# Constant exponential scale from powers of two on q and k, and a reordered front, in an attention and mixture-of-experts kernel

## The reference, cut to what matters

```python
x  = L0_attn_x                     # (B, S, D) = (4, 1024, 128)
xn = layernorm(x, eps=1e-5)
Q = rope(heads(xn @ W_q.T));  K = rope(heads(xn @ W_k.T));  V = heads(xn @ W_v.T)   # 16 heads of 8
attn = softmax(Q @ K.T / sqrt(8))  # full, 1024 x 1024 for each head
a = merge(attn @ V) @ W_o.T
# feed-forward: 8 experts, the top 2 for each row of xn
w, idx = top_k(xn @ Wg, 2);  w = softmax(w)
h_e = relu((norm(xn) * gamma_e + beta_e) @ W1_e + b1_e)
f = sum over the two experts of w_e * (h_e @ W2_e + b2_e + xn)
out = x + a + f
```

## Time and profile before

| | |
|---|---|
| median of 3 runs | 660.07 us (659.75 to 661.24) |
| the profiled execution: time | 659.6 us |
| its span | 657.7 us |
| PE busy | 608.5 us (93%) |
| ACT busy | 548.6 us (83%) |
| DVE busy | 384.1 us (58%) |
| POOL busy | 226.1 us (34%) |

### The profile page before, as it was taken

One profiled execution on the slowest core, in us unless ns is written; L12 is line 12 of the kernel. 1 busy time (PEld: TensorE's weight loads), 2 busy tenths in 40 slices (PEclk: granted clock), 3 DMA queues, 4 the chain that ended last, 5 costly groups with the idle time before them and its releaser, 6 DMA issues.

```text
span 657.7 us, 12339 instructions
## 1 busy us (share of the span) xinstructions
PE 608.5 (93%) x4649; PEld 256.8 (39%) x4649; DVE 384.1 (58%) x1117; ACT 548.6 (83%) x552; POOL 226.1 (34%) x261
## 2 busy tenths in 40 slices
PE   8789889988999999999999999999999999888884
PEld 6223312213545454434454545443444545111112
DVE  4854687888555555587655555558765564335112
ACT  2678899998788888888888888888888888999993
POOL 4399900027753433332433343333234221100000
PEclk9989999999999999999999999999999999999997
DMA  6156411002201202000220120200012111530000
GB/s 229 27 164 179 117 32 33 1 9 53 61 18 29 57 29 57 25 21 17 57 62 17 30 57 29 57 25 21 17 53 54 29 21 45 225 137 32 1 1 34
DMA packets 25425, 35.60 MB, mean 54 GB/s; under 512 B 5472, under 2 KB 15760, under 8 KB 24848
## 3 DMA queue, kind: packets, MB, share of 16 engines
q1 hardware_dynamic: 19936, 23.70, 11.9%
q0 software_dynamic: 4608, 9.45, 5.0%
q10 hardware_dynamic: 816, 1.61, 0.7%
HBM read 17.43 MB, written 8.91 MB: 40 GB/s over the span
## 4 chain that ended last, share of the span: by engine, by line
PE 63%; ACT 22%; DVE 8%; issue 2%; SPq 2%; DMA 1%; DVEq 1%; POOL 0%; ACTq 0%
PE acc L613 23%; ACT ring L825 22%; PE bank L665 11%; PE sc L580 11%; PE bank L657 9%; PE bank L650 2%; PE bank L511 2%; SPq L303 2%; PE bank L674 1%; DVE xn L1169 1%; DVE turned L1148 1%; DVE work L1182 1%; DVE rotated L867 1%; DMA wr<-L_attn_W_k 1%; DVE hl L863 1%
## 5 line engine op out<-in xcount | busy, mean ns | idle before, releaser
L825 ACT ACTIVATE ring<-sc,exp_scale 128x1024 f32<-128x1024 f32 x512 | 534.5, 1130 | 83.2 <-PE sc L580 82.3
L613 PE MATMUL acc<-ring,v 128*9 128x512 f32 x2048 | 268.8, 597 | 2.5 <-issue 2.5
L580 PE MATMUL sc<-qs,ks 32*128 32x512 f16 x1024 | 147.2, 386 | 28.6 <-ACT ring L825 27.4
L456 POOL DMA_INDIRECT token_out<-work,token x72 | 78.4, 1089 | 155.4 <-DVE work L1189 149.1
L446 POOL DMA_INDIRECT work<-normed,token x72 | 70.1, 973 | 159.2 <-DVE work L1175 95.0
L580 PEld LDWEIGHTS sc<-qs,ks 32*128 32x128 f16 x1024 | 40.0, 91 | 145.3 <-ACT ring L825 110.7
L665 PEld LDWEIGHTS bank<-xn,work 128*128 128x128 f32 x576 | 69.7, 191 | 65.1 <-DVE work L1182 37.7
L1182 DVE TENSOR_SCALAR work<-bank,xn 128x128 f32<-128x128 f32 x288 | 80.9, 343 | 22.9 <-PE bank L657 22.8
L665 PE MATMUL bank<-xn,work 128*128 128x128 f32 x576 | 83.2, 287 | 3.1 <-DVE work L1175 3.0
L657 PE MATMUL bank<-work,xn 128*128 128x128 f32 x576 | 77.2, 277 | 2.1 <-DVE norms L888 1.3
L1169 DVE COPY xn<-w_all 128x1158 f32 x72 | 56.5, 785 | 33.2 <-DVE work L1189 32.3
(11 more groups left out here) (175 smaller groups left out, 336.5 us busy)
## 6 DMA issues: line engine op xcount, KB each, us to landing
w_all<-L_ffn_W SPq DMA_DIRECT2D x16, 256.0 KB, 4.9
qs<-hl SPq DMA_DIRECT2D x60, 64.0 KB
ks<-hl SPq DMA_DIRECT2D x60, 64.0 KB
x<-L_attn_x SPq DMA_DIRECT2D x4, 512.0 KB, 7.9
normed<-xn SPq DMA_DIRECT2D x4, 512.0 KB, 3.3
xn<-token_out SPq DMA_DIRECT2D x2, 1024.0 KB, 6.8
w_all<-token_out SPq DMA_DIRECT2D x2, 1024.0 KB, 11.6
out<-x SPq DMA_DIRECT2D x8, 256.0 KB, 2.3
```

Source lines behind the costliest of these rows:

```text
L456: pool.indirect_dma_start(out=y_d[:, :], in_=ys[done % TILE_BUFFERS], in_offset=None, out_offset=bass.IndirectOffsetOnAxis(ap=token[:, 1, ...
L580: last = nc.tensor.matmul(dst, ks[r:r + 32, kb * P:(kb + 1) * P], qs[r:r + 32, at], start=True, stop=not slow)
L613: last = nc.tensor.matmul(acc[qh % 2][32 * j:32 * j + VW, :], v9[:, b, kb, 4 * g + j, :], ring[:, (2 * n + j // 2) % UNITS, j % 2, :], sta ...
L825: nc.scalar.activation(ring[:, (2 * n + u) % UNITS, :, :], sc[u][:, :].rearrange("p (h c) -> p h c", h=2), ACT.Exp, scale=exp_scale[:, 0:1 ...
```

## The change

Both powers of two are now chosen so that their product is 2^14 where there is room for it. The exponential's scale is then the constant 1/(sqrt(8)·2^14), written into the instruction. `exp_scale`, `ungain` and `bound_scale` are gone. `missing` is the factor that k lacks where there was no room; then `no_room` makes the first flag zero, and the general path, which has an additional copy of q and k in `wide`, multiplies what is missing. Its scores run on `wide`.

Beside that the front is reordered: fewer warm-up matmuls; of piece 0 the plain projection comes before the rotated one, for PE and for DVE; the rotated projection of piece 3 comes behind the head norms; the plain projection of piece 2 is made before the flag is read, not in step 0; the moments of batches 2 and 3 are taken at steps 3 and 5; the top-2 of the first batch at step 8 and not 4. POOL makes -mean/std for each row (`offsets`, two small operations) and norms rows as x·a + b; it clears `shift` at the very start, and sorts `wo` before the low halves. `gates` has one operation less.

```diff
-GAIN_EXPONENT = 127 + 12 + 63
+SCORE_BITS = 14
+TOP_EXPONENT = 127 + 12 + 63
-WARM = (10, 18)
+WARM = (10, 12)
-TOP_AT = {4: 0, 11: 1, 15: 2, 19: 3}
+MOMENTS_AT = {3: 2, 5: 3}
+TOP_AT = {8: 0, 11: 1, 15: 2, 19: 3}
...
# POOL
+            nc.gpsimd.memset(shift[:, :], 0.0).then_inc(shift_zero, 1)
...
+            def offsets(ts):
+                after(nc.gpsimd.tensor_tensor(small[:, 9, ts], mv[:, ts, 0], small[:, 6, ts], ALU.mult))
+                after(nc.gpsimd.tensor_scalar(small[:, 8, ts], small[:, 9, ts], -1.0, None, ALU.mult))
...
-                nc.gpsimd.tensor_scalar(xn[:, t, :], x[:, t, :], mv[:, t, 0:1], small[:, 6, t:t + 1],
-                                        ALU.subtract, ALU.mult).then_inc(xn_pool, 1)
+                nc.gpsimd.tensor_scalar(xn[:, t, :], x[:, t, :], small[:, 6, t:t + 1], small[:, 8, t:t + 1],
+                                        ALU.mult, ALU.add).then_inc(xn_pool, 1)
...
# PE, the front
-            for r in range(2):
-                project_front(sc[r][:, CH:2 * CH], r, 1).then_inc(proj, 1)
-                project_front(sc[r][:, 0:CH], r, 0).then_inc(proj, 1)
+            project_front(sc[0][:, 0:CH], 0, 0).then_inc(proj, 1)
+            project_front(sc[0][:, CH:2 * CH], 0, 1).then_inc(proj, 1)
+            project_front(sc[1][:, CH:2 * CH], 1, 1).then_inc(proj, 1)
+            project_front(sc[1][:, 0:CH], 1, 0).then_inc(proj, 1)
...
+            pe.wait_ge(rope_rot, 1)
             project_front(sc[0][:, 0:CH], 2, 0).then_inc(proj, 1)
-            project_front(acc[1][:, :], 3, 1).then_inc(proj, 1)
             values(0, 1)
             pe.wait_ge(head_ok, 1)
             head_norms(0)
+            project_front(acc[1][:, :], 3, 1).then_inc(proj, 1)
             values(0, 2)
             check_bound(0)
             values(0, 3)
+            project_plain()
             pe.wait_ge(rope_out, 2)
...
# ACT
-            act.wait_ge(scale_ok, 2)
...
-                                         ACT.Exp, scale=exp_scale[:, 0:1]).then_inc(e_ok, 1)
+                                         ACT.Exp, scale=SCALE / (1 << SCORE_BITS)).then_inc(e_ok, 1)
...
# DVE
-                nc.vector.tensor_scalar(gain[:, :].bitcast(I32), half_exp[:, :], -float(1 << 23),
-                                        float(GAIN_EXPONENT << 23), ALU.mult, ALU.add).then_inc(gain_ok, 1)
+                nc.vector.tensor_scalar(room[:, :], half_exp[:, 0:1], float(127 + SCORE_BITS - 12 - 63), None,
+                                        ALU.add)
+                link(nc.vector.tensor_scalar(gain_exp[:, :], half_exp[:, :], -1.0, float(TOP_EXPONENT), ALU.mult,
+                                             ALU.add))
+                link(nc.vector.tensor_tensor(gain_exp[:, 1:2], gain_exp[:, 1:2], room[:, :], ALU.min))
+                nc.vector.tensor_scalar(gain[:, :].bitcast(I32), gain_exp[:, :], float(1 << 23), None, ALU.mult
+                                        ).then_inc(gain_ok, 1)
...
+            def missing_gain():
+                link(nc.vector.tensor_tensor(no_room[:, :], room[:, :], gain_exp[:, 1:2], ALU.subtract))
+                nc.vector.tensor_scalar(missing[:, :].bitcast(I32), no_room[:, :], 127.0, float(1 << 23), ALU.add,
+                                        ALU.mult)
+                link(nc.vector.tensor_scalar(no_room[:, :], no_room[:, :], 0.0, None, ALU.is_le))
...
             def turn_front(i, r, plain_of, plain_made, rotated_of, rotated_made):
-                v.wait_ge(proj, rotated_made)
-                times(rotated[:, :], rotated_of, r, sin)
+                if rotated_made < plain_made:
+                    v.wait_ge(proj, rotated_made)
+                    times(rotated[:, :], rotated_of, r, sin)
                 v.wait_ge(proj, plain_made)
                 v.wait_ge(sq_ok, i + 1)
                 times(turned[r % 2][:, :], plain_of, r, cos).then_inc(rope_out, 1)
+                if rotated_made > plain_made:
+                    v.wait_ge(proj, rotated_made)
+                    times(rotated[:, :], rotated_of, r, sin).then_inc(rope_rot, 1)
+                    v.wait_ge(rope_rot, 1 if i == 0 else 2)
                 add_up(i, r)
...
-            scales()
+            missing_gain()
             bound(0)
             decide(0)
...
-            for b in range(1, B):
+            def moments_of(b):
                 v.wait_ge(x_in[b], 16)
                 moments(range(TB * b, TB * (b + 1)))
+            moments_of(1)
```

More of the change, by code:

```diff
@@ L178, in build @@
         w_norm, half_exp = sb("w_norm", [P, 2]), sb("half_exp", [P, 2], I32)
-        gain, ungain, exp_scale, bound_scale = (sb(n, [P, 2]) for n in ("gain", "ungain", "exp_scale", "bound_scale"))
+        gain_exp, gain = sb("gain_exp", [P, 2]), sb("gain", [P, 2])
+        room, missing, no_room = (sb(n, [P, 1]) for n in ("room", "missing", "no_room"))
+        wide = [sb(f"wide_{n}", [P, S], F32R) for n in ("q", "k")]
         w_all = sb("w_all", [P, E, W_LEN])
@@ L282, in build @@
         y_out = [sem(f"y_out{k}") for k in range(TILE_BUFFERS)]
-        m_mm, m_red, m_tr, m_chain, m_split, m_in = ([sem(f"{n}{b}") for b in range(B)] for n in
-                                                     ("m_mm", "m_red", "m_tr", "m_chain", "m_split", "m_in"))
+        m_wide, m_mm, m_red, m_tr, m_chain, m_split, m_in = (
+            [sem(f"{n}{b}") for b in range(B)] for n in
+            ("m_wide", "m_mm", "m_red", "m_tr", "m_chain", "m_split", "m_in"))
         block = ctx.enter_context(nc.Block())
@@ L408, in _ @@
             pool.wait_ge(rstd_ok, 2)
+            offsets(slice(0, TB))
             for t in range(4, TB):
                 normed(t)
+            pool.wait_ge(wo_in, 16)
+            pool.wait_ge(wqk_tr, 1)
+            pool.wait_ge(w_sq_ok, 2)
+            nc.gpsimd.tensor_copy(wo_by_head[:, :].rearrange("o (j g d) -> o j g d", j=4, g=4),
+                                  wr[:, 3, :].rearrange("o (g j d) -> o j g d", g=4, j=4)).then_inc(wo_sorted, 1)
             for i, r in enumerate((0, 3, 2)):
@@ L425, in _ @@
                 pool.wait_ge(rstd_ok, b + 2)
+                offsets(ts)
                 for t in range(TB * b, TB * (b + 1)):
@@ L588, in maxima @@
                 b, base = q // 4, q % 4
-                qs, ks = stack[q % 2]
+                qs, ks = wide
                 wait(pe, e_ok, 2 * PER_QUAD * q)
+                pe.wait_ge(m_wide[b], 2 * (base + 1))
                 pe.wait_ge(shift_zero, 1)
@@ L955, in _ @@
             split_high(2).then_inc(high_ok, 1)
-            for b in range(1, B):
+            def moments_of(b):
                 v.wait_ge(x_in[b], 16)
                 moments(range(TB * b, TB * (b + 1)))
+            moments_of(1)
             def maxima(q):
                 b, base = q // 4, q % 4
+                wait(v, s_mm, 2 * PER_QUAD * q)
+                if q == 0:
+                    v.wait_ge(first_in, 16 * 2 * COPIES)
+                    v.wait_ge(later_q_in, 16 * COPIES)
+                v.wait_ge(stack_in[q % 2], loads_into(q % 2, q // 2 + 1))
+                qs, ks = stack[q % 2]
+                nc.vector.tensor_scalar(wide[0][:, :], qs[:, :], missing[:, :], None, ALU.mult).then_inc(m_wide[b], 1)
+                nc.vector.tensor_copy(wide[1][:, :], ks[:, :]).then_inc(m_wide[b], 1)
                 for n in range(4 * TB):
@@ L1036, in gates @@
             def gates():
-                v.wait_ge(rstd_ok, B + 1)
-                link(nc.vector.scalar_tensor_tensor(out=small[:, 8, :], in0=mv[:, :, 0], scalar=-1.0,
-                                                    in1=small[:, 6, :], op0=ALU.mult, op1=ALU.mult))
+                v.wait_ge(xn_pool, T - 4)
                 v.wait_ge(gate_exp, 1)
```

35 lines of the change are left out of this document (11 added, 24 removed).

## The result

The changed kernel takes 636.43 us (median of 4 runs, 635.86 to 637.09) against 659.91 (4 runs, 658.87 to 661.24) for the kernel before on the same chip: a ratio of 0.9643, 95% interval 0.9623 to 0.9664. The forecast was 635.7 (631 to 650). The profiled execution took 636.86 us, with a span of 635.0; that is 22.7 less than the span of before. One thing has to be known for the front: the point from which TensorE's clock is recorded at full speed varies between executions, from 4.0 to 10.5 us in 14 profiles. It does so without any difference in the instructions: in after it is 10.1 us, in two kernels that differ from after only from step 216 on it is 4.0 and 6.4. In the profiled execution of before it is 4.6.

A forecast was written before the change was run, and what follows sets the result against it. Limits differ by stretch: ACT's exponentials in ACT-only stretches with PE close behind, PE among the experts with waits for exponentials. Savings 2.5 + 5.0 + 10.4 + 6.2 + 0.3 = 24.4 us, 660.07 to 635.7, range 631 to 650.

The forecast's parts named there:

- The size of the exponential's saving: Each exponential without its scale tensor: 0.100 us less latency and 0.090 less spacing, bounds 0 and 0.117.
- Before the experts: Attention steps from 45 to 160 us: shorter exponentials in chain pieces and runs save 5.0 us.
- Experts: Steps with experts: 55 long chain pieces of scores give back 0.19 us each, 10.4 us; bounds 0 and 14.4.
- Last stretch: Last 40 attention-only steps: from 2.01 to 1.855 us each, PE's loop taking over as limit, 6.2 us.
- The front: Start of the kernel up to step 6: the reordering brings L626 from 41.45 to 38.95, worth 2.5 us.
- What follows keeps its length: Front, behind DVE's second product at 26.4: sum, halves, twelve issues and small loads last as before, L626 at 38.95.
- The clock after the stall: Behind PE's stall at step 5: the 1.2 GHz stretch stays; without it the gain would be 1 to 1.5 us larger.
- A scale tensor that costs nothing: Rival on the exponentials: removing their scale tensor saves nothing, only the front's gain is left, 657.5 us; chance 0.08.
- a saving of latency only: Rival on the exponentials: latency falls but spacing does not, saving 9.2 us in all, so 651 us; chance 0.10.
- The general path: Rival: `no_room` is 0 and every batch runs with maxima, over 1400 us in all on DVE; chance 0.01.
- The sign of a late POOL: Sign of a wrong forecast: a new stall of PE at steps 13 to 15, waiting for POOL's rows; priced under 1 us.
- a front that gives back its gain: Rival before the projections: shorter warm-up leaves PE at 1.2 GHz, price 1 to 3 us, time near 638; chance 0.05.

The follow-up runs named there:

- half-column kernel: The kernel after with the weigh matmuls of steps 216 to 255 over 256 of the 512 columns: 644.17 us, ratio 0.9755 to the kernel before.
- half-`weigh` kernel: The kernel after with two of the four heads' weigh matmuls left out from step 216 on: 636.34 us, ratio 0.9627 to the kernel before.

## Why the prediction was right, and where it was off

**What bounds the kernel: right.** Three stretches with three limits, read from windows and chains, were confirmed by taking the constant away in two of them.

**The size of the exponential's saving: right.** Taken from the square's row: 0.100 off the latency and 0.090 off the spacing. Measured: 0.090 off the latency (1.113 to 1.023) and 0.092 off the least spacing (0.995 to 0.903). The square was the nearest row and a good one; the copy gave 0.117, more than was there to be had.

**Before the experts: 5.0 forecast, 4.76 measured** (steps 7 to 54; with the tensor everywhere, 107.45 us again). **Experts: 10.4 forecast, 10.07 measured** (steps 54 to 214), and 9.9 when the tensor was put back there alone. Counting the long scores in the chain, and giving each 0.19, was the right way; multiplying 0.20 by 72 tiles would have given 14.4.

**Last stretch: 6.2 for 40 steps forecast, 5.8 measured** (from step 214 to 254, 81.3 to 75.5 us; the tensor put back gave 6.0). The loop over two steps takes 3.720, forecast 3.71. The pattern of the spacings is 0.966, 0.920, 0.914, 0.920; the long one starts some 0.04 behind the end of its scores, the others at ACT's own distance. So the wait for PE that I forecast is there, but it is a sliver of 0.05 in two steps, and the chain view does not show it: it still has one run of exponentials, where I had expected pieces of scores and weigh between them. That sign was wrong: two limits that lie within 0.06 us of each other over two steps can't be told apart in the chain. That the loop, and not ACT, sets it, rests on this pattern, on the half-column kernel, in which the same spacing is 0.912, and on the half-`weigh` kernel, in which it is 0.952.

**The front: 2.5 forecast, 1.3 in the profiled execution.** By the medians with the tensor put back it is worth 2.2, near the forecast, but part of that agreement is luck: three of four profiles of the old front lose time to a low clock that the profile I forecast from does not show (below), and the forecast had no term for it. The forecast had the flag at 22.15, the first exponential at 24.0 and L646 at 38.95; they came at 22.96, 24.74 and 40.14. Three terms of it:

- *"Six fewer warm-up matmuls let PE's transposes and projections start earlier, by about 1.2 us."* At the low clock up to 10.1 us they started at 11.27, 0.4 later than in before. DVE's first product then waited 1.02 us for ACT's square of the late projection, the wait that I had taken away:

```profile
11.27 0.60 PE L509 MATMUL bank<-const,xn 128*128 128x128 f32 x4
...
13.09 0.17 DVE L895 TENSOR_SCALAR gain<-gain_exp 128x2 int32<-128x2 f32 x1
14.28 0.75 DVE L883 SCALAR_TENSOR_TENSOR turned<-sc,gain,cos 128x512 f32<-128x512 f32 x1 [1.02 <-ACT oT L822]
```

  This is the execution and not the edit. In the five profiles that have PE's front of after and an early full clock, DVE's first step waits for the `sin` table, as I had forecast, and not for ACT later (rows of the kernel with the tensor in the experts' steps):

```profile
12.17 0.16 DVE L891 TENSOR_SCALAR w_norm<-acc 128x2 f32<-128x2 f32 x1 [1.71 <-DMA sin<-rope_sin]
13.23 0.75 DVE L886 SCALAR_TENSOR_TENSOR turned<-sc,gain,cos 128x512 f32<-128x512 f32 x1
```

  In these five the flag comes at 21.35 to 22.23 (22.15 forecast) and the first exponential at 23.14 to 24.03 (24.0 forecast). The latest of them had its table 0.6 us or more after the others. In the two with the low clock in the warm-up (after, and its half-`weigh` kernel) DVE waits 1.02 and 1.16 us for ACT, and the flag comes at 22.96 and 23.68. In the six profiles that have the whole front of after, L646 comes at 38.64 to 40.55 (38.95 forecast), in the four with the old front at 41.45 to 42.48.
- The flag's transpose: I did not cost what the reordered PE program puts ahead of it, a projection of 1.05 and `values` of 0.47. But this had cover: moved forward, it brought the flag 1.3 us earlier and the first exponential not at all.
- *"What follows keeps its length"*: DVE's second product ends at 27.2 (it starts at 26.48), where the forecast had 26.4: 0.8 late, as much as the flag. The gain on before (28.90) is 1.7. The low half on POOL ends at 29.64, but the twelve issues start at 29.89, only 1.46 earlier than in before (31.35), because piece 3's own four issues on SP, one of them 1.11 long, end at 29.84. That is another 0.2, in the queue that I moved the step past and did not walk through. L646 follows SP's queue to the end: 1.31 earlier than in before. Of the missing 1.2 us in this profile, 0.8 are thus the late flag, which by the seven profiles above goes with the low clock, and some 0.25 SP's queue.

**The clock after the stall: forecast to stay, and it did.** It stood at half speed (1.2 GHz) around or behind the stall in all eleven profiles in which PE was idle there for 1.6 to 2.9 us; it did not fall in the one with 1.2 us of idle time and in the two without a stall. I had priced its removal at 1 to 1.5 us; removal of stall and low clock together measured 3.6. Of this some 0.9 is the clock from step 7 on, by the steps 7 to 54 above; the rest I can't divide.

**Rivals.** A scale tensor that costs nothing, and a saving of latency only, are refuted by the spacing and by the constant put alone into before. The general path was not taken: DVE's groups hold no reductions of 1024 columns. The sign of a late POOL was not seen either: between the steps 8 and 54 of after PE is never idle for more than 0.8 us at a time. The rival of a front that gives back its gain was partly seen: PE was at the low clock up to 10.1 us. Its first exponential came 0.7 to 1.6 us later than in the five profiles above, near the low end of the rival's price of 1 to 3, but not for its reason, since the low clock lay in the warm-up itself and ended before the first projection (10.1 us; the transposes began at 11.27), and the longer warm-up gave no earlier first exponential.

**One gain that the forecast did not have.** In three of four profiles with the old front (the constant in before, and both half-`weigh` kernels made from before) the clock fell to half speed at 25 to 27 us, for 3.4 or 6.8 us; step 2 then came 1.3 to 2.3 us later than in before's profile, and step 7 still 0.7 to 1.3 us later; the rest vanished in the stall of step 5. The profile of before is the fourth, without it. In none of ten profiles with the new front did this happen. PE is busy for 3.47 of the 4 us from 20 to 24 in after, and for 2.03 in before, since the rotated projection of piece 3 and most of the plain one of piece 2 now stand there. That this is the cause is argued, not shown.

## What to carry to other kernels

In a hot loop, an activation's scale that is a constant in the code instead of a tensor shortens it here by 0.09 us in latency and in spacing, and was worth 20 of 660 us; make the varying part a power of two in the data, and check in the chain what the loop has left: in stretches whose chain names only PE, 10 of these 20 us were to be found in the waits between PE's own matmuls. When a step is moved, walk every queue behind it up to the next stall: the one that sets it (here three small loads behind twelve issues of 0.6 us) is often cheaper to move than the step. And work that is free because its engine waits is free only as long as it waits.

## What the runs showed of the hardware

- Less work on PE, slower kernel: `weigh` over 256 of 512 columns in the last stretch was followed by half the clock for 71.7 us (in before's version for 78.5), and the kernels took 7.7 and 5.9 us more.
- Four `weigh` matmuls of 9 rows of output run side by side: two instead of four save 0.014 us of 0.979.
- Half a clock of 3.4 us behind a stall goes with 0.9 us more from step 7 to 54, 6.8 us with 1.8 to 1.9.
- The start of the full clock moved between 4.0 and 10.5 us from execution to execution, while PE's first instructions were the same; one profile lost it again from 7.4 to 10.8 us, in the middle of the warm-up.
- The operand's price was 0.090 and 0.092 us. The page "ScalarE: Activation LUTs" of the Trainium skill, section "What ACT_TABLE_LOAD costs", gives about 93 ns for each pointer operand; the runs agree. They do not agree with the spacing that follows from its figures, an estimate of 1.04 us with the operand and 0.946 without: measured are 1.005 on average in the last stretch of before (0.996 to 1.012), and 0.903 to 0.920 in after where ACT does not wait.
